# Pacing the table gathers of a recommendation tower by finished work, with other weights in the planner of its order

## What is computed

```python
e = jnp.stack([tbl_0[ids[:, 0]], ..., tbl_31[ids[:, 31]]], axis=1)   # 1024 x 32 x 64
left = jnp.einsum('bpd,pde->bpe', xi, W)                            # xi = e[:, i], 496 pairs
z = jnp.sum(left * xj, axis=-1)
h = jnp.concatenate([z, dense_ctx], axis=1)
h = jnp.maximum(h @ W_top1 + b_top1, 0.0)
h = jnp.maximum(h @ W_top2 + b_top2, 0.0)
y = h @ W_top3
```

## Time and profile before

| | us |
|---|---|
| median of three runs | 724.18 |
| own time of the profiled execution | 729.45 |
| its span, first to last instruction | 727.7 |
| TensorE matmul busy | 418.7 |
| VectorE busy | 327.3 |
| ScalarE busy | 351.9 |
| GpSimd busy | 292.2 |

### The profile page before, as it was taken

How to read it: one execution, slowest core, us unless ns; L and a number is a source line. 1 busy time by engine, 2 the same in 40 slices (tenths; PEclk the granted TensorE clock), 3 DMA queues, 4 the chain that set the end, 5 groups by cost and what they waited for, 6 DMA issues and landing times.

```text
span 727.7 us, 8998 instructions
## 1 busy us (share of the span) xinstructions
PE 418.7 (58%) x2440; PEld 217.8 (30%) x2440; DVE 327.3 (45%) x285; ACT 351.9 (48%) x2639; POOL 292.2 (40%) x350
## 2 busy tenths in 40 slices
PE   0400040003599894312199999433209999999988
PEld 0200020000245551000056555210005555455545
DVE  0000000000399891100099998300017998987771
ACT  0000011002599995100378997410008898998852
POOL 6777777772000007777300000777720000565330
PEclk9955555556599998555599999855558999999999
DMA  9996311110000001111000000111100000000000
GB/s 143 174 169 97 77 26 27 27 25 9 1 1 2 1 1 26 25 28 25 13 1 2 2 1 1 25 26 26 27 11 3 1 1 1 3 2 2 1 1 1
DMA packets 44681, 18.88 MB, mean 26 GB/s; under 512 B 39764, under 2 KB 40280, under 8 KB 44632
## 3 DMA queue, kind: packets, MB, share of 16 engines
q1 hardware_dynamic: 36120, 8.86, 9.2%
q0 software_dynamic: 8512, 9.45, 7.0%
HBM read 18.29 MB, written 0.00 MB: 25 GB/s over the span
## 4 chain that ended last, share of the span: by engine, by line
PE 38%; another core or an unknown queue 34%; issue 14%; ACT 10%; DVE 2%; POOL 0%; POOLq 0%; DVEq 0%; ACTq 0%
PE left L798 12%; PE left L793 11%; ACT row_products L690 9%; PE z_sum L819 6%; PE turned L837 3%; PE turned L859 2%; PE turned L758 1%; PE left L806 1%; PE left L837 1%; DVE row_products L645 1%; ACT X L673 1%; DVE column_products L637 1%; POOL row_products L595 0%; PE left L859 0%
## 5 line engine op out<-in xcount | busy, mean ns | idle before, releaser
L578 POOL DMA_INDIRECT rows<-in_tbl_dram,ids_sb x256 | 242.3, 947 | 285.4 <-DVE row_products L645 206.2
L690 ACT ACTIVATE row_products<-row_products 128x64 f32<-128x64 f32 x1280 | 306.8, 247 | 58.2 <-issue 53.4
L690 ACT ACTIVATION_READ_ACCUMULATOR row_products<-row_products 128x1 f32 x1280 | 248.2, 194 | 42.0 <-issue 42.0
L637 DVE TENSOR_TENSOR column_products<-left,X 128x1024 f32<-128x1024 f32 x104 | 124.2, 1217 | 210.8 <-remote 130.1
L798 PE MATMUL left<-w_sb,X 64*128 64x512 f32 x480 | 131.8, 641 | 119.0 <-issue 118.5
L645 DVE TENSOR_TENSOR row_products<-left,rows 128x1024 f32<-128x1024 f32 x120 | 143.2, 1218 | 101.0 <-remote 68.1
L793 PE MATMUL left<-X,w_sb 64*128 64x256 f32 x960 | 137.1, 417 | 72.3 <-issue 35.3
L793 PEld LDWEIGHTS left<-X,w_sb 64*128 64x128 f32 x960 | 97.0, 203 | 128.2 <-issue 62.0
L673 ACT ACTIVATE X<-turned 128x512 f32<-128x512 f32 (+1 forms) x34 | 19.2, 565 | 210.1 <-remote 173.6
L819 PE MATMUL z_sum<-column_products,ones_window 128*32 128x512 f32 x512 | 79.6, 642 | 33.4 <-issue 23.3
L595 POOL TENSOR_TENSOR row_products<-row_products 128x512 f32<-128x512 f32 (+4 forms) x70 | 42.5, 607 | 123.9 <-DVE row_products L645 119.5
(11 more groups left out here) (30 smaller groups left out, 87.7 us busy)
## 6 DMA issues: line engine op xcount, KB each, us to landing
rows<-in_tbl_dram,ids_sb POOLq DMA_INDIRECT x256
w_sb<-in_W_top_dram SPq DMA_DIRECT2D x1, 512.0 KB
w_sb<-in_L_rec_W_dram SPq DMA_DIRECT2D x1, 496.0 KB
w_sb<-in_L_rec_W_dram SPq DMA_DIRECT2D x1, 480.0 KB
w_sb<-in_L_rec_W_dram SPq DMA_DIRECT2D x1, 464.0 KB
w_sb<-in_L_rec_W_dram SPq DMA_DIRECT2D x1, 448.0 KB
w_sb<-in_L_rec_W_dram SPq DMA_DIRECT2D x1, 432.0 KB
w_sb<-in_L_rec_W_dram SPq DMA_DIRECT2D x1, 416.0 KB
```

What stands on the lines that cost most here:

```text
L578: pool.indirect_dma_start(out=rows[:, q % 2 * QT + t, f * D:(f + 1) * D], out_offset=None, in_=tables[f], in_offset=bass.IndirectOffsetOnA ...
L637: nc.vector.tensor_tensor(to, of, X[:, n:n + 2, :].rearrange("p g b -> p (g b)").unsqueeze(1).to_broadcast([P, 2, BANK]), ALU.mult).then_i ...
L690: ins = nc.scalar.activation(product, product, ACT.Copy, accum_out=z_nat[:, tile, column:column + 1])
```

## The change

Each gather of a pair of fields from n = 13 on waits, on GpSimd, until `int(3.4 * (n - 12))` pieces are multiplied: 3 pieces for n = 13, 6 for n = 14, 68 for n = 32, 173 for n = 63. The waits at the heads of quarters 2 and 3 stay. The planner's `landed` takes the new waits into account, and three of its weights and one limit are others.

```diff
-MLP_APART = 6
+MLP_APART = 4
-WORK, OWN, SUM, SET, TRANSPOSE, LAYER, SWITCH, RELOAD = 0.87, 1.85, 0.215, 0.15, 0.12, 1.72, 0.1, 0.12
+WORK, OWN, SUM, SET, TRANSPOSE, LAYER, SWITCH, RELOAD = 0.85, 1.85, 0.215, 0.15, 0.12, 1.72, 0.1, 0.12
-ACT_SLACK, DVE_SLACK, MARGIN, NEAR, LAST_LEAD, POOL_AFTER = 1.5, 0.6, 1.0, 0.3, 0.15, 4.0
+ACT_SLACK, DVE_SLACK, MARGIN, NEAR, LAST_LEAD, POOL_AFTER = 0.5, 0.6, 1.0, 0.3, 0.1, 4.0
+PACED, PIECES_APART = 12, 3.4
+
+def pieces_before(q, m):
+    n = FP * q + FP - 1 - m
+    return max(0, int((n - PACED) * PIECES_APART))
...
     def landed(self, q, m):
-        if q < 2:
-            return GATHER * (FP * q + FP - m) + LANDING
-        if not self.done(q - 2):
-            return None
-        begin = max(GATHER * FP * q, max(e for e, x in zip(self.end, self.work) if x[1] == q - 2))
-        return max(begin + GATHER * (FP - m), GATHER * (FP * q + FP - m)) + LANDING
+        end = GATHER * (FP * q + FP - m)
+        if q >= 2:
+            if not self.done(q - 2):
+                return None
+            end = max(end, max(e for e, x in zip(self.end, self.work) if x[1] == q - 2) + GATHER * (FP - m))
+        for n in range(m, FP):
+            if pieces_before(q, n) > len(self.end):
+                return None
+            if pieces_before(q, n):
+                end = max(end, self.end[pieces_before(q, n) - 1] + GATHER * (n - m + 1))
+        return end + LANDING
...
                 for m in range(FP - 1, -1, -1):
+                    if pieces_before(q, m):
+                        pool.wait_ge(multiplied, pieces_before(q, m))
                     for t in range(QT):
                         for f in (2 * m, 2 * m + 1):
                             pool.indirect_dma_start(
```

## The result

| | before | changed |
|---|---|---|
| median, us (lowest to highest; runs) | 724.09 (722.9 to 725.5; 4) | 584.62 (583.82 to 586.02; 4) |
| ratio, 95% interval | | 0.8075, 0.8052 to 0.8098 |
| profiled execution: own time, span, us | 729.45, 727.7 | 586.02, 584.1 |

A forecast was written before the change was run, and what follows sets the result against it. Gather bursts under which the other engines crawl, half of the 727.7 us span, were taken to decide. 78 + 50 x 6.55 + 5.6 + 111.4 + 1.5 + 22.9 = 546.9 us span, so 545 us median; range 490 to 725.

The forecast's parts named there:

- the crawl: Dark stretches under long gather bursts: other engines nearly stop, signals stuck behind a queue taking 1.41 us a gather; 367.15 us together.
- T: Period from one paced group of four gathers to the next: 5.05 + 1.5 = 6.55 us, bounds 5.64 and 10.7.
- the forecast case: T from 5.64 to 7.5 us, span 501 to 594 us, median 498 to 592; chance 0.52.
- The first paced gather: End of the 52 unpaced gathers of the first 13 pairs, taken as 78 us, bounds 69 and 83.
- The 50 periods: From the first paced gather to the last group's, between 51 groups: 50 x 6.55 us.
- After the last release: 75 pieces left at 1.485 us, 111.4 us, plus 1.5 us of the last group's crawl and the 22.9 us end.
- The 4.1 us: Full work continuing from a group's start before the crawl, mean of three marks at 272.89; named likeliest to be wrong.
- The waits behind: TensorE's waits for rows at its turns: costed at nothing, since release comes 27 to 40 pieces ahead; otherwise 5 to 10 us.
- Only partly spared: Rival: short groups leave the queue warm, T 7.5 to 10 us, span 594 to 719 us; chance 0.20.
- Cost nothing: Rival: gathers in short groups cost nothing and the queue's rate doesn't bind, T 5.05 to 5.64, span 472 to 501; chance 0.10.
- Slower, the full 1.41 us for each however short the burst: Rival: every queued gather stops the work for 1.41 us, T 10.7 us, span 753, median 750; chance 0.15.
- Nothing changes: Rival: the waits are met already or the dark stretches have another cause, about 724 us; chance 0.03.

The follow-up runs named there:

- The finer grain: The changed kernel with one wait before each single gather instead of before each group of four; on chip 5 562.46 us, ratio 0.7734.

## Why the prediction was right, and by how much off

Direction and mechanism were right: long bursts bring the crawl, waits on the pieces break them up, and T lies in the forecast case. One term was too small, and the case was nearly missed (T = 7.46 with 7.5 as its end). It is luck that the comparison met a crawl as the trace had: on chip 7 the same change gives 426.08 us, far below the range. The terms in order:

- **The first paced gather**, forecast at 78 us, came at 77.24: -0.8 us. The row of the waits has it behind VectorE's L655, as forecast.
- **The 50 periods.** The last group starts at 455.92; (455.92 - 77.24 - 5.6) / 50 = 7.46 us, against T = 6.55. That is +45.6 us and more than the whole error: T was mis-sized by 14%, still inside the forecast case (up to 7.5). The prediction itself put some 9 us on the bunching at quarter 3 and left them out of its sum.
- **After the last release** 584.1 - 455.9 = 128.2 us, against 111.4 + 1.5 + 22.9 = 135.8: -7.6 us. The 75 pieces took (128.2 - 22.9) / 75 = 1.40 us each with all crawl behind the last group in it, 1.485 was forecast.
- **The sum:** -0.8 + 45.6 - 7.6 = 37.2 us = 584.1 - 546.9. The weights were costed at 0 with bounds of 5 us; on chips 7 and 12 they give 0.4 to 0.5% or some 2 us. Their share on a chip that crawls was not measured.
- **One reading**, the last gather of the second burst issued at 353.6, is about 1 us late: it starts at 351.70. Nothing in the sum rests on it.

**What was wrong in T.** The step that failed is "the crawl takes the remaining 5.64 - 4.1 = 1.5 us of each period", with its premise that the period settles itself, one group after the other. It doesn't: a release is met by pieces that come in spurts, and 34 runs of the queue hold the 208 gathers. A second group that follows without a pause has, by the same reasoning, no 4.1 us unharmed in front of it; it costs its full 5.64. Worked out with the true issue times the crawl is 208 x 1.41 - 34 x 4.1 = 154 us, where the forecast has about 51 x 1.5 = 77. The measured loss is between them: 378.7 us less 170 pieces at 1.485 (252.5) is 126 us, against 50 x 6.55 + 5.6 - 252.5 = 80.6 by the forecast. So the reckoning by runs overshoots, by 28 us. Two things stand behind that number. Much work gets through in these short crawls: 42 pieces in 148 us, against 23 in the 367 us of before, so that of the 126 us only some 85 are lost in them. And 41 are lost outside them, where the forecast lost nothing. The finer grain on chip 5 has 79 and 28. The clock has a part in the second. It stands at 0.87 in the second stretch, where I wrote "near 1.00", and a matmul record takes 292.75 / 1664 = 0.176 us there and 243.38 / 1632 = 0.149 in the run without a crawl. Those are some 45 us more of TensorE busy. The granted clock is at its lower level, 0.50 or 1.2 GHz, for 97.5 of the 378.7 us, 76 of them outside the reckoned crawls. One such stretch follows the stop at 282.0 (columns as in the earlier trace rows):

```profile
294.20:301.00 6.80, 6.11 (x18) 3.07 (x20) 4.97 (x5) 2.99 (x23) 3.77 (x4) 0.50 0.07 14
```

With the factor of 1.6 of the earlier trace rows, 76 us at the lower level do the work of 47, so the clock could account for up to 29 of the 41 us. This is an estimate; it takes TensorE as the bound in all of them, which no run tests.

**The 4.1 us**, named as the weakest point, held where it was asked about, soon after a burst. At 277.75 VectorE goes on for 4.25 us, though the queue had been empty only since 271.45 + 4 x 1.41 = 277.09. It is no constant: at 357.34 VectorE goes on for 7.59 us.

**The waits behind** were costed at nothing, and there is no wait for rows at L776. The paced start at the sixth pair shows that this was a cover and not a matter of course. The head of quarter 3 was forecast to bunch three groups; it bunched four, and the idle of VectorE behind them, 15.11 us, is the only one above 10 from 80 us on.

**What the profile was to show:** waits for L663 and L655 "some 50 times" are 30 (18 and 12), groups 6 to 7 us apart are 5.0 to 19.4 apart with a mean of 7.57 (7.46 less W_top1's part), and the last gather came at 459.67, not at 400 to 415. All three are the same error, the uneven releases.

**The rivals.** *Only partly spared* (T 7.5 to 10) is missed by 0.04 us; the traces give another reason than its own, runs and a lower clock and no warm queue. *Cost nothing* is excluded by the stands of 7.10 and 15.11 us. *Slower, the full 1.41 us for each however short the burst*, falls: a gather took 1.28 us of the others' time before (1.41 less 23 x 1.485 / 260), takes (7.46 - 5.05) / 4 = 0.60 in the changed kernel, and (7.20 - 0.11 - 5.05) / 4 = 0.51 with a wait before each, where the 0.11 is W_top1's 5.6 us over 50. *Nothing changes* was right in a way that I hadn't thought of: on chips 7 and 12 the waits don't bind. My reason against it, only 2 pieces done at 68.65, holds for a trace with a crawl alone. The step from "this trace" to "this kernel" was never questioned. On chip 7 the change is worth 0.5%, not 19%, and on chip 12 neither of its parts is worth more.

By the Trainium skill's page "SBUF — State Buffer", section "Who interferes with whom", TensorE and ScalarE never wait for another engine's access. On chips 7 and 12 nothing contradicts it: both work on under continuous gathers (TensorE for 243.38 and ScalarE for 230.88 of 245.80 us in the kernel before on chip 7). In the first comparison both nearly stand still under the same gathers, so the rule is no ground for a forecast there.

**Open.** What makes a chip crawl, and whether it is the chip or a state of it. The queue of 1.41 us is inferred from the times at which work resumes (289.03 and 289.11, 379.9 and 380.03); no record shows it. The trace of before says two things of what it is not. The rows themselves are not late. The last gather of the second burst starts at 351.70, and this is the traffic after it (last column, GB/s), before and, after the last gather at 327.03, on chip 7:

```profile
353.00:354.00 1.00, 0.58 (x1) 0.00 (x0) 0.00 (x0) 0.26 (x1) 0.00 (x0) 0.50 0.16 33
354.00:355.00 1.00, 0.00 (x0) 0.28 (x1) 0.00 (x0) 0.00 (x0) 0.00 (x0) 0.50 0.00 0
...
330.00:331.00 1.00, 0.88 (x10) 0.46 (x8) 0.81 (x1) 1.00 (x10) 0.84 (x3) 1.00 0.00 0
```

Both are done some 3 us after the issue, and the crawl goes on until 362.8. Nor is it only the signals between engines that are slow, as the prediction reads it. In the same tail ScalarE's own steps within one row sum, which wait for no other engine, start 0.70 us apart, half of 1.41, and 0.09 to 0.16 us apart once the crawl is over:

```profile
360.04 0.26 ACT L690 ACTIVATE row_products<-row_products 128x64 f32<-128x64 f32 x1 [0.51 <-issue]
360.73 0.20 ACT L690 ACTIVATION_READ_ACCUMULATOR row_products<-row_products 128x1 f32 x1 [0.43 <-issue]
361.43 0.26 ACT L690 ACTIVATE row_products<-row_products 128x64 f32<-128x64 f32 x1 [0.50 <-issue]
...
363.23 0.19 ACT L690 ACTIVATION_READ_ACCUMULATOR row_products<-row_products 128x1 f32 x1
```

And the record is thinner where the kernel crawls. The view of the DMAs has a time to landing for the gathers on chip 7 (second line, 2.4 us) and none before (first line):

```profile
rows<-in_tbl_dram,ids_sb POOLq DMA_INDIRECT x256
...
rows<-in_tbl_dram,ids_sb POOLq DMA_INDIRECT x256, 2.4
```

The traces hold 701 landing events for the kernel before and 1510, 1413 and 1999 for the three paced ones that crawled, against 4659 to 4804 in every run that didn't, the plain DMAs on chip 5 among them. So whether the recording of events has a part in the crawl is an open rival that no run tests. Not measured on a chip that crawls were also the waits without the weights, the weights without the waits, groups of sixteen, and consecutive rows. That the waits and not the new order bring the 19% there is argued: from the pauses of GpSimd in the trace, and from the 0.5% that the order gives elsewhere.

## What to carry to other kernels

Lookups by indirect DMA in a long burst held up all engines on some chips. Releasing them by finished work, 27 to 40 pieces ahead of their use, took 19% off there in groups of four and 23% one by one. Where there is no crawl the waits alone took nothing off and cost nothing (0.9998 and 1.0007). When you forecast a pace, ask how unevenly the work that releases it arrives: count how many transfers lie in one run, not only how far apart they are in the mean, and ask what the clock does after each stop. And a stall in a profile belongs to the chip of that profile until a second chip shows it.

## What the hardware showed that I had not expected

- The same program takes 724 to 727 us on some chips and 428 on others. Runs taken together kept to one or the other: 7 runs of before at 726.05 to 729.16 on chip 5, and medians of 427.76 and 428.38 in the two sets on chip 7.
- On the chip that crawled, 256 indirect DMAs in bursts cost some 315 us (726.83 - 411.96) over plain ones of the same bytes at consecutive addresses. On chip 7, without a crawl, the kernel with the indirect ones takes 16 us more than that (428.38 - 411.96).
- The crawl outlasts the traffic and the issue, one instruction at a time (0.70 us from one step of ScalarE to the next), and ends when a queue of 1.41 us for each gather would be empty, though the issue takes 1.25 us and is the same on both kinds of chip (944 to 947 ns busy).
- Plain DMAs from GpSimd are issued one in 0.53 us on chip 5, indirect ones one in 1.25 (945 ns and 0.3 of pause) on every chip.
- After a stop the granted clock can be at its lower level, 1.2 GHz, while the engines work again (0.50 from 294.2 to 301.0), so a stop can cost more than its own length.
